# Gates' second half from high and low parts, the ends of two stages reordered, and the first mixture's gathers in another order

## The chip, the cores and the metric

One core of a Trainium2 chip runs the whole program. The metric is the device time of one execution in microseconds (us). TensorE (PE) multiplies, VectorE (DVE), ScalarE (ACT) and GpSimd (POOL) do the rest, SyncE (SP) issues transfers; ScalarE and GpSimd issue some too.

## What is computed

The reference is a chain of six layers on 2048 rows of 256 features, each added to its input: a cross-attention, a delta-rule layer, a mixture of 8 experts, and a second cross-attention, self-attention and mixture. The change touches the second and the third. Cut to what matters:

```python
# L0_attn, the delta-rule layer
q, k, v = (silu(causal_conv(h @ W, conv)) for W, conv in ...)
beta = sigmoid(h @ W_b)
delta_out = delta_rule_chunkwise(q, k, v, beta)      # chunks of 32 rows
fir_s, fir_l = causal_conv(v, short), causal_conv(v, long)
gate_in = concat([h, fir_s, fir_l, delta_out], -1)   # 1024 features
hid = gelu(gate_in @ W_fuse1 + b_fuse1)              # 512 features
logits = (hid @ W_fuse2 + b_fuse2).reshape(b, l, H, 4)
p_raw = sigmoid(logits[..., 3])
floor = 0.01 + 0.09 * (1 - p_raw)
p_val = (1 - floor) * p_raw
others = softmax(logits[..., :3] / exp(others_log_tau))
o = mix of fir_s, fir_l, delta_out, v by others and p_val;  rmsnorm;  @ W_o
# L0_ffn, the first mixture: top 2 of 8 experts, per expert
y = silu(x @ W1[e]) @ W2[e]
```

## The kernel before

Each stage is a block: all engines meet at its end, and within it they run queues written out by hand and held together by semaphores. All sums are kept in f32. PE's matmuls take f32 operands, or, in other stages, a number is split into a high part (rounded to fp32r) and a low part (the rest, in fp32r), and `product3` (L124) makes three fp32r products in place of one f32 product. The copy that rounds is done by ScalarE or GpSimd, the subtraction that leaves the low part mostly by VectorE.

**Work taken ahead.** Layer 4's keys and values for its 64 batches are formed ahead, beside other stages, in parts: three for a batch (`KeysAhead`, from L317; matmuls at L386 and L390, evictions on ScalarE at L410 and L412, then a store, for which the place two batches later waits). `ahead.pe(e, n)` puts n parts into PE's queue, `ahead.act(e, n)` n evictions into ScalarE's. Two banks are used in turn. In the text such a part is a kv part.

**The front of the delta rule** (`delta_attention`, from L992): projections, convolutions, then the norms of q and k in four groups: squares on GpSimd (L1136), sums by PE (`norms`, L1089), a copy by ScalarE (`normed`, L1149), turned by PE (`norms_back`, L1098), taken by VectorE (L1221), square roots on ScalarE (L1199, L1201), reciprocals and two products on VectorE (L1240 to L1248). PE ends with four matmuls without use that keep its clock (L134).

**The solve** (`delta_solve`, from L1256). VectorE solves the triangular systems of 32 rows in two halves, with the taps of the long convolutions (L972) between the steps. SP brings the matrix back turned, in eight loads a half (L1320). PE's queue after the gram matrices is: 14 kv parts, `fuse_most(0)`, 8 kv parts, `half_outputs(0)`, `fuse_rest(0)`, `fuse_most(1)`, `fuse_rest(1)`, 4 kv parts, `fuse_most(2)`, `half_outputs(1)`, `logits(0)`, `fuse_rest(2)`, `fuse_most(3)`, `fuse_rest(3)`, `logits(1)`. `fuse_most(g)` makes, for 512 rows, the first 6 of the 8 chunks of 128 features of gate_in @ W_fuse1, for 4 banks of 128 outputs (L1369, 24 matmuls of 128x512 f32), `fuse_rest(g)` the last 2 (L1375, 8 matmuls), which need the delta rule's output. In the trace each such f32 matmul stands as two records. `half_outputs` multiplies the turned matrix with v (L1350), `hidden(g)` on ScalarE applies gelu (L1438).

**The gates** (`mixture_gates`, from L1524): 16 small steps of VectorE and ScalarE, with 4 kv parts on PE.

**The first mixture** (`experts_0`, from L1740). 23 blocks of rows, in the order narrow (128 rows), wide, wide (256), seven times, and then wide ones. GpSimd gathers for each block 1 MB of W1 (`gather1`, L1849) and 1 MB of W2 (`gather2`, L1855) by the block's expert, and the rows (`gather_rows`, L1868, 128 KB for each half block), all in one queue. For wide blocks GpSimd makes the high part of W1 (`high1`, L1862), VectorE the low one (`low1`, L2077); W2's are made by ScalarE (L2030) and VectorE (`low2`, L2081). There are two slots for the weights and four for the rows. PE turns the rows (L1930) and multiplies with W1 (`hidden`, or `hidden_narrow`, L1942) and W2 (`outputs`). In the text w1(j), w2(j) and rows(j) are the gathers of block j.

## Time and profile before

| | |
|---|---|
| median of 3 runs | 1607.41 us (1605.9 to 1612.63) |
| the profiled execution | 1609.45 us, its span 1607.6 us |
| PE busy | 1484.7 us, 92% of the span |
| VectorE busy | 1097.5 us, 68% |
| ScalarE busy | 813.4 us, 51% |
| GpSimd busy | 586.0 us, 36% |
| mean granted PE clock | 0.986 |
| DMA | 203.99 MB, mean 127 GB/s |

The span runs from the first to the last instruction. Busy time is the time in which at least one instruction of the engine ran. "idle before" names the time that an engine stood before an instruction, and what ended it. A line such as `f_xg<-rows,f_token` gives the output tile and the inputs. The page's clock row, in 40 slices of 40 us, has 9 (nine tenths or more) in all slices but one, which has 8 and begins at 1326 us.

### The profile page before, as it was taken

How to read it: one execution, taken by the hardware profiler on the slowest of the kernel's cores; microseconds unless marked ns; L12 is line 12 of the kernel's file. 1: busy time of each engine (PE TensorE's matmuls, PEld its weight loads, DVE VectorE, ACT ScalarE, POOL GpSimd, SP SyncE). 2: the span in 40 equal slices, each digit the busy share in tenths (PEclk: the TensorE clock that was granted, in tenths of full speed). 3: DMA queues.
4: the chain of work that ended last, by engine and by line, in shares of the span. 5: the costliest groups of instructions: out<-in, count | busy, mean ns of one | idle time of the engine just before them, and what ended most of it. 6: DMA issues, size and time to landing. Idle time of an engine off the chain costs nothing. (4 is left out here: it accounts for less than half of the span.)

```text
span 1607.6 us, 38476 instructions
## 1 busy us (share of the span) xinstructions
PE 1484.7 (92%) x15176; PEld 1139.9 (71%) x15176; DVE 1097.5 (68%) x2412; ACT 813.4 (51%) x1849; POOL 586.0 (36%) x487
## 2 busy tenths in 40 slices
PE   6898989999988889999999889999899788999998
PEld 4454467555456579999998756666688686799997
DVE  4588879973057455566562568888699676767887
ACT  1234742121134336666563548999377322766663
POOL 2440310000011035677654256787388452121210
PEclk9999999999999999999999999999999998999999
DMA  9992059522023367677657417664000000010001
GB/s 321 359 342 74 1 180 215 125 62 46 1 96 122 112 216 253 220 255 253 246 183 189 131 50 245 207 205 135 28 1 1 24 24 15 1 34 21 27 1 53
DMA packets 114075, 203.99 MB, mean 127 GB/s; under 512 B 38074, under 2 KB 74362, under 8 KB 108010
## 3 DMA queue, kind: packets, MB, share of 16 engines
q1 hardware_dynamic: 91481, 107.72, 23.0%
q0 software_dynamic: 10032, 57.55, 10.4%
q10 hardware_dynamic: 12384, 36.27, 6.8%
q8 instruction: 122, 2.00, 0.5%
q14 instruction: 56, 0.45, 0.1%
HBM read 161.67 MB, written 39.83 MB: 125 GB/s over the span
## 5 line engine op out<-in xcount | busy, mean ns | idle before, releaser
L2390 POOL TENSOR_TENSOR a_pr<-a_pr,a_inv 128x1028 f32<-128x1028 f32 x64 | 122.1, 1908 | 58.7 <-DVE a_inv L2523 58.6
L386 PE MATMUL ps<-kv_ctx,kv_w 128*128 128x257 f32 x464 | 120.6, 395 | 9.5 <-PEq L1841 3.1
L2485 ACT ACTIVATE a_pr<-ps,a_neg 128x257 f32<-128x257 f32 x256 | 119.0, 473 | 18.9 <-DVE a_neg L2539 18.8
L390 PE MATMUL ps<-kv_w,kv_ctx 128*128 128x256 f32 x464 | 114.4, 390 | 12.1 <-ACT kv_kv L410 11.5
L1631 POOL TENSOR_TENSOR b0m_pm<-b_dr,b_gates 128x256 f32<-128x256 f32 x16 | 13.2, 831 | 280.5 <-SPq L1595 251.5
L2539 DVE TENSOR_REDUCE a_neg<-ps 128x2 f32<-128x514 f32 x128 | 87.8, 688 | 37.4 <-PE ps L2407 36.4
L390 PEld LDWEIGHTS ps<-kv_w,kv_ctx 128*128 128x128 f32 x464 | 86.7, 193 | 32.3 <-ACT kv_kv L410 20.1
L3401 DVE SCALAR_TENSOR_TENSOR x<-ps,g_gate,x 128x256 f32<-128x256 f32 x256 | 105.1, 475 | 0.0
L386 PEld LDWEIGHTS ps<-kv_ctx,kv_w 128*128 128x128 f32 x464 | 85.5, 195 | 27.5 <-issue 15.0
L972 DVE SCALAR_TENSOR_TENSOR b_F<-b_F,b_fir 128x992 f32<-128x992 f32 (+29 forms) x128 | 96.5, 789 | 0.0
L2418 PE MATMUL ps<-ident,a_pr 128*128 128x128 f32 x512 | 80.4, 279 | 16.0 <-ACT a_prT L2492 10.6
L126 PE MATMUL ps<-gw_w1H,g_hH 128*128 128x256 f32 x320 | 90.6, 283 | 0.8 <-DVE x L3401 0.8
L128 PE MATMUL ps<-gw_w1H,g_hL 128*128 128x256 f32 x320 | 90.5, 283 | 0.0
L127 PE MATMUL ps<-gw_w1L,g_hH 128*128 128x256 f32 x320 | 90.5, 283 | 0.0
L2418 PEld LDWEIGHTS ps<-ident,a_pr 128*128 128x128 f32 x512 | 53.9, 141 | 51.0 <-issue 48.6
L126 PE MATMUL ps<-f_w2H,f0w_hH 128*128 128x256 f32 x312 | 88.6, 284 | 0.2 <-DVE f_w2L L2081 0.2
L128 PE MATMUL ps<-f_w2H,f_hL 128*128 128x256 f32 x312 | 87.9, 282 | 0.0
L127 PE MATMUL ps<-f_w2L,f0w_hH 128*128 128x256 f32 x312 | 87.4, 280 | 0.0
L3371 DVE TENSOR_TENSOR g_hL<-g_hr,g_hH 128x512 fp32r<-128x512 f32 x80 | 57.4, 719 | 39.2 <-ACT g_hH L3339 39.0
L410 ACT ACTIVATE kv_kv<-ps,kv_bk 128x257 f32<-128x257 f32 x92 | 42.5, 471 | 71.6 <-PE ps L386 53.7
L126 PE MATMUL ps<-f_xTH,f0w_w1H 128*128 128x256 f32 x256 | 73.3, 286 | 5.3 <-issue 5.3
L3331 ACT ACTIVATE g_r<-ps 128x512 f32<-128x512 f32 x80 | 47.7, 596 | 53.5 <-PE ps L128 53.5
(448 smaller groups left out, 4431.6 us busy)
## 6 DMA issues: line engine op xcount, KB each, us to landing
late_kv<-kv SPq DMA_DIRECT2D x52, 513.0 KB, 4.1
kv<-kv_kv ACTq DMA_DIRECT2D x46, 513.0 KB
a_ctxT<-in_ctxT SPq DMA_DIRECT2D x32, 514.0 KB, 8.8
a_ctxR<-in_ctx SPq DMA_DIRECT2D x32, 512.0 KB
kv_ctx<-in_ctxT ACTq DMA_DIRECT2D x34, 257.0 KB
kv_ctx<-in_ctxT SPq DMA_DIRECT2D x24, 257.0 KB
outs<-f_yo SPq DMA_DIRECT2D x16, 256.0 KB
a_vB<-vlast SPq DMA_DIRECT2D x32, 128.0 KB
```

What stands on the lines that cost most here:

```text
L126: e.matmul(out, wh, xh, start=start, stop=False)
L127: e.matmul(out, wh, xl, start=False, stop=False)
L128: return e.matmul(out, wl, xh, start=False, stop=stop)
L386: done = e.matmul(out[:, 0:NK], self.w[:, 0, c, cols(part)], ctx[:, c, :], start=(c == 0), stop=(c == DC - 1))
L390: done = e.matmul(out[:, cols(t, D)], ctx[:, c, cols(t)], self.w[:, 1, c, :], start=(c == 0), stop=(c == DC - 1))
L972: return e.scalar_tensor_tensor(acc, x, fir[:, src, at - 1 - sh:at - sh], acc, ALU.mult, ALU.add)
L2390: e.tensor_tensor(pr[:, b % RP, :, :], pr[:, b % RP, :, :], inv[:, b % 2, :].unsqueeze(2).to_broadcast([P, HG, NK]), ALU.mult).then_inc(*p ...
L2418: done = e.transpose(K.ps[:, 6, cols(r)], pr[:, b % RP, r, cols(t)], K.ident[:, :])
L2485: e.activation(pr[:, b % RP, r, :], K.ps[:, bank(b, r), 0:NK], ACT.Exp, bias=neg[:, b % 2, r:r + 1], accum_out=tot[:, b % 2, r:r + 1]).the ...
L2539: e.tensor_reduce(neg[:, b % 2, r:r + 2], K.ps[:, at:at + 2, 0:NK], AX.X, ALU.max, negate=True).then_inc(*v_mx.up())
L3371: e.tensor_tensor(h[1][:, n % HS, :], hr[:, n % 2, :], h[0][:, n % HS, :].bitcast(F32), ALU.subtract).then_inc(*v_l.up())
L3401: done = e.scalar_tensor_tensor(K.x[:, row, :], K.ps[:, 4 + 2 * (m % 2) + half, cols(t, D)], gate[:, row, x - SH:x - SH + 1], K.x[:, row, ...
```

## The change

- The front's end: the sixth kv part comes before `norms(3)` on PE, both last evictions before `normed(3)` on ScalarE, and VectorE's `norms(3)` before the first reciprocal.
- The solve: W_fuse1 is split into `f1H` and `f1L`, and gate_in's chunks for g = 2 and 3 into the two slots of `parts`; for these groups `fuse_parts` makes 3 fp32r matmuls of 128x512 in place of each f32 one, chunk by chunk with the four banks inside (before: bank by bank with the chunks inside). `f1H` takes the place of the keys after the gram matrices, `f1L` that of `f1`, `parts` that of the first two groups of `xnT`. So low parts of the weights can only be made after `fuse_rest(1)`. PE has 12 kv parts before `fuse_most(0)` and 6 after `fuse_rest(1)` (before: 14 and 4).
- Tau's exp and reciprocal move from the gates block to the end of the solve block; the sigmoid becomes exp(-x), + 1, reciprocal.
- The first mixture: GpSimd's queue begins w1(0), w2(0), rows(0), w1(1), rows(1) (before: w1(0), w1(1), w2(0), rows(0), rows(1)).

```diff
@@ delta_attention, tensor
                     norms_back(2)
-                    A.pe(e, 2)
+                    A.pe(e, 3)
                     norms(3)
-                    A.pe(e, 1)
                     norms_back(3)
@@ scalar
-                    A.act(e, 1)
+                    A.act(e, 2)
                     normed(3)
-                    A.act(e, 1)
@@ vector
                     norms(2)
+                    norms(3)
                     e.wait_ge(*a_root.at(1))
                     e.reciprocal(rn[:, 0:12, :], rn[:, 0:12, :]).then_inc(*v_inv.up())
-                    norms(3)
@@ delta_solve, helpers
+        def part(n):
+            return [parts[:, w, cols(n % 2, 512)] for w in range(2)]
+        def low_weights(e, k):
+            if k == 0:
+                e.wait_ge(*a_wh.at(8))
+                e.wait_ge(*t_h.at(8))
+            e.tensor_tensor(f1L[:, k, :], f1[:, k, :], f1H[:, k, :].bitcast(F32), ALU.subtract).then_inc(*v_wl.up())
+        def low_source(e, n):
+            high, low = part(n)
+            e.wait_ge(*a_sh.at(n + 1))
+            e.tensor_tensor(low, source(n % 8, 2 + n // 8), high.bitcast(F32), ALU.subtract).then_inc(*v_sl.up())
@@ tensor
+                def fuse_parts(first, last):
+                    for n in range(first, last):
+                        g, k = 2 + n // 8, n % 8
+                        e.wait_ge(*v_sl.at(n + 1))
+                        if g == 2:
+                            e.wait_ge(*v_wl.at(k + 1))
+                        for m in range(4):
+                            if k == 0:
+                                e.wait_ge(*a_h.at(4 * g + m - 3))
+                            done = product3(e, K.ps[:, m, :], [w[:, k, cols(m)] for w in (f1H, f1L)], part(n), k == 0, k == 7)
+                            if k == 7:
+                                done.then_inc(*t_h.up())
+                        if k < 7:
+                            done.then_inc(*t_k.up())
-                ahead.pe(e, 14)
+                ahead.pe(e, 12)
-                ahead.pe(e, 4)
-                fuse_most(2)
+                ahead.pe(e, 6)
+                fuse_parts(0, 6)
                 ahead.wait_taken(e)
                 half_outputs(1)
                 e.wait_ge(*v_o.at(NT))
                 logits(0)
-                fuse_rest(2)
-                fuse_most(3)
-                fuse_rest(3)
+                fuse_parts(6, 16)
                 logits(1)
@@ scalar
+                def high_source(n):
+                    g, k = 2 + n // 8, n % 8
+                    if n == 0:
+                        e.wait_ge(*t_h.at(8))
+                    if n >= 2:
+                        u = n - 2
+                        if u % 8 == 7:
+                            e.wait_ge(*t_h.at(4 * (2 + u // 8) + 4))
+                        else:
+                            e.wait_ge(*t_k.at(u + 1 - u // 8))
+                    if 2 <= k < 6:
+                        e.wait_ge(*v_fir.at(2 * len(FIR_TAPS)))
+                    if k == 6:
+                        e.wait_ge(*a_oT.at(4 * g + 4))
+                    e.activation(part(n)[0], source(k, g), ACT.Copy).then_inc(*a_sh.up())
-                ahead.act(e, 50)
+                ahead.act(e, 40)
+                e.wait_ge(*ld_f.at(16))
+                e.wait_ge(*t_G.at(NT))
+                for k in range(8):
+                    e.activation(f1H[:, k, :], f1[:, k, :], ACT.Copy).then_inc(*a_wh.up())
+                    ahead.act(e, 1)
...
+                hidden(0)
+                hidden(1)
+                high_source(0)
+                high_source(1)
+                ahead.act(e, 6)
+                for n in range(2, 6):
+                    high_source(n)
+                for t in range(H2, NT):
+                    turned_o(t)
+                for n in range(6, 9):
+                    high_source(n)
+                hidden(2, (0, 1))
+                high_source(9)
+                hidden(2, (2, 3))
+                for n in range(10, 16):
+                    high_source(n)
+                hidden(3)
                 e.wait_ge(*t_lg.at(2))
                 e.activation(lgraw, K.ps[:, 4, :], ACT.Copy).then_inc(*a_raw.up())
+                e.activation(tau[:, :], ltau[:, :], ACT.Exp).then_inc(*a_tau.up())
@@ vector
                 fir_taps(2 * len(FIR_TAPS))
+                for n in range(6):
+                    low_weights(e, n)
+                    low_source(e, n)
+                for k in (6, 7):
+                    low_weights(e, k)
                 for t in range(H2, NT):
                     outputs(t)
+                for n in range(6, 16):
+                    low_source(e, n)
@@ mixture_gates, scalar
-                e.activation(tau[:, :], ltau[:, :], ACT.Exp).then_inc(*a_tau.up())
-                e.activation(raw[:, :, :], lg[:, :, :, 3], ACT.Sigmoid).then_inc(*a_sig.up())
+                e.activation(raw[:, :, :], lg[:, :, :, 3], ACT.Exp, scale=-1.0).then_inc(*a_sig.up())
@@ vector
                 e.wait_ge(*a_sig.at(1))
+                e.tensor_scalar(raw[:, :, :], raw[:, :, :], 1.0, None, ALU.add).then_inc(*v_one.up())
+                e.wait_ge(*v_one.at(1))
+                e.reciprocal(raw[:, :, :], raw[:, :, :]).then_inc(*v_sig.up())
@@ experts_0, gpsimd
                 gather1(0)
-                gather1(1)
+                gather2(0)
                 e.wait_ge(*st_r.at(16 * NT))
-                gather2(0)
                 e.wait_ge(*v_token.at(1))
                 gather_rows(0)
+                gather1(1)
                 gather_rows(1)
                 high1(1)
```

## Rows read from the trace of the kernel before

**Rows 1.** Timeline of TensorE at the front's end: start, duration, what, idle before.

```profile
208.83 1.06 PE L1089 MATMUL ps<-b0a_sq,masks 128*32 128x512 f32 x8 [2.38 <-issue]
...
211.66 0.60 PE L1098 MATMUL ps<-ident,b0a_norm 128*128 128x128 f32 x4
...
216.72 0.26 PE L1334 MATMUL ps<-b_qk 64*32 64x32 f32 x5 [1.02 <-PEq L1033]
```

**Rows 2.** Timeline of TensorE in the solve block.

```profile
292.28 1.99 PE L390 MATMUL ps<-kv_w,kv_ctx 128*128 128x256 f32 x8 [0.54 <-ACT kv_kv L410]
...
330.17 1.93 PE L1350 MATMUL ps<-b_dr,b0s_AS 32*32 32x64 f32 x64 [1.09 <-ACT kv_kv L412]
...
373.72 1.90 PE L386 MATMUL ps<-kv_ctx,kv_w 128*128 128x257 f32 x8
...
378.05 1.88 PE L1369 MATMUL ps<-b_xnT,b0s_f 128*128 128x512 f32 x4
...
398.74 1.10 PE L1350 MATMUL ps<-b_dr,b0s_AS 32*32 32x64 f32 x64
```

**Rows 3.** Timeline of SyncE's queue: the eight loads of the turned matrix, first half.

```profile
317.39 7.22 SPq L1320 DMA_DIRECT2D b0s_AS<-turned  x8
```

**Rows 4.** View of line L1320: time from issue to landing, 16 loads.

```profile
DMA to landing us min/median/max: 2.2/3.6/4.3
```

**Rows 5.** Timeline of TensorE in the last mixture, three fp32r matmuls of 128x512 apart.

```profile
1402.06 0.40 PE L126 MATMUL ps<-g_xnH,gw_w1H 128*128 128x512 f32 x1
...
1402.75 0.28 PE L126 MATMUL ps<-gw_w1H,g_hH 128*128 128x256 f32 x1
```

**Rows 6.** Groups by line and shape: count | busy us, mean ns | idle before.

```profile
L3371 DVE TENSOR_TENSOR g_hL<-g_hr,g_hH 128x512 fp32r<-128x512 f32 x80 | 57.4, 719 | 39.2 <-ACT g_hH L3339 39.0
...
L3339 ACT ACTIVATE g_hH<-g_hr 128x512 fp32r<-128x512 f32 x80 | 50.6, 633 | 2.6
```

**Rows 7.** Timeline of ScalarE and TensorE in the gates block.

```profile
450.91 1.28 ACT L1543 ACT_TABLE_LOAD   x1 [1.52 <-PEq L1301]
...
456.22 3.24 PE L386 MATMUL ps<-kv_ctx,kv_w 128*128 128x257 f32 x8 [2.44 <-ACT kv_kv L410]
...
460.28 0.84 PE L1603 MATMUL ps<-ident,b_F 128*128 128x128 f32 x6 [0.82 <-PEq L1536]
```

**Rows 8.** Timeline of GpSimd in the first mixture.

```profile
593.93 1.89 POOL L1862 CAST f0w_w1H<-f_raw 128x2048 fp32r<-128x2048 f32 x1 [1.70 <-DMA f_raw<-in_L_ffn_W1T,f_wrow]
595.98 3.08 POOL L1868 DMA_INDIRECT f_xg<-rows,f_token  x1 [0.16 <-issue]
...
606.35 0.94 POOL L1849 DMA_INDIRECT f_raw<-in_L_ffn_W1T,f_wrow  x1 [4.80 <-PE ps L1942]
...
612.69 1.90 POOL L1862 CAST f0w_w1H<-f_raw 128x2048 fp32r<-128x2048 f32 x1 [4.14 <-DMA f_raw<-in_L_ffn_W1T,f_wrow]
...
638.49 1.01 POOL L1849 DMA_INDIRECT f_raw<-in_L_ffn_W1T,f_wrow  x1 [0.30 <-issue]
...
646.38 1.89 POOL L1862 CAST f0w_w1H<-f_raw 128x2048 fp32r<-128x2048 f32 x1 [3.94 <-DMA f_raw<-in_L_ffn_W1T,f_wrow]
...
678.08 1.91 POOL L1862 CAST f0w_w1H<-f_raw 128x2048 fp32r<-128x2048 f32 x1 [4.99 <-DMA f_raw<-in_L_ffn_W1T,f_wrow]
```

**Rows 9.** Timeline of TensorE in the first mixture.

```profile
599.04 0.69 PE L1930 MATMUL ps<-ident,f_xg 128*128 128x128 f32 x2 [7.23 <-DMA f_xg<-rows,f_token]
...
632.72 3.74 PE L1942 MATMUL ps<-f_xN,f_raw 128*128 128x128 f32 x32
...
663.00 3.74 PE L1942 MATMUL ps<-f_xN,f_raw 128*128 128x128 f32 x32
...
714.33 0.36 PE L126 MATMUL ps<-f_xTH,f0w_w1H 128*128 128x256 f32 x1 [1.42 <-issue]
```

**Rows 10.** Timeline of VectorE beside the second row of rows 8.

```profile
595.92 2.29 DVE L2077 TENSOR_TENSOR f0w_w1L<-f_raw,f0w_w1H 128x2048 fp32r<-128x2048 f32 x1 [6.38 <-POOL f0w_w1H L1862]
```

**Rows 11.** Busy time by stretch: PE, PEld, DVE, ACT, POOL, granted clock, DMA.

```profile
327.00:329.00 2.00, 2.00 (x6) 1.11 (x4) 0.00 (x0) 0.00 (x0) 0.00 (x0) 0.52 0.47 127
```

More of the change, by code:

```diff
@@ L996, in delta_attention @@
         sb = Y.sb
-        xnT = sb("xnT", [P, DC, ROWS])
+        with Room(Y, "b0x") as Z:
+            xnT = Z.sb("xnT", [P, DC, ROWS])
+        parts = sb("parts", [P, DC, ROWS], F32R)
+        with Room(Y, "b0k") as Z:
+            kk = Z.sb("kk", [P, 2, ROWS])
+        f1H = sb("f1H", [P, 8, 512], F32R)
         wo = sb("wo", [P, DC, D])
@@ L1250, in delta_attention, with delta_solve @@
         K.front.Y.close()
-        delta_solve(K, A, a_first, xnT, qk, F, fir, dr, rn, cb, ab, f2, bf1, bf2, lg, ld_2)
-        mixture_gates(K, A, lg, gates, ltau)
+        tau = sb("tau", [P, H0])
+        delta_solve(K, A, a_first, tau, ltau, xnT, parts, qq, kk, f1H, F, fir, dr, rn, cb, ab, f2, bf1, bf2, lg, ld_2)
+        mixture_gates(K, A, lg, gates, tau)
         delta_mix(K, A, F, dr, gates, wo, nw)
-def delta_solve(K, ahead, a_first, xnT, qk, F, fir, dr, rn, cb, ab, f2, bf1, bf2, lg, ld_2):
+def delta_solve(K, ahead, a_first, tau, ltau, xnT, parts, qq, kk, f1H, F, fir, dr, rn, cb, ab, f2, bf1, bf2, lg, ld_2):
     H2 = NT // 2
@@ L1266, in delta_solve @@
         step = sb("step", [P, L * L // 4])
-        f1 = sb("f1", [P, 8, 512])
+        with Room(Y, "b0f") as Z:
+            f1 = Z.sb("f1", [P, 8, 512])
+        f1L = sb("f1L", [P, 8, 512], F32R)
         ld_f, d_AS, d_Mt = Y.sigs_of("dma", "f1 AS Mt")
+        a_wh, a_sh = Y.sigs_of("act", "fhigh shigh")
+        v_wl, v_sl, t_k = Y.sig("dve", "flow"), Y.sig("dve", "slow"), Y.sig("pe", "chunk")
         ld_A, d_M = ([Y.sig("dma", f"{n}{h}") for h in range(2)] for n in "AM")
@@ L1333, in grams @@
                             out, col = K.ps[L * b:L * b + L, 2 * s + h % 2, :], L * (h // 2)
[L1334 removed]
+                            e.matmul(out[:, col:col + L], kk[rows, h // 2, at], kk[rows, h // 2, at],
                                      start=True, stop=True)
[L1336 removed]
+                            e.matmul(out[:, P + col:P + col + L], kk[rows, h // 2, at], qq[rows, h // 2, at],
                                      start=True, stop=True)
@@ L1427, in _, with hidden @@
             def _(e):
+                def high_source(n):
[13 more added lines that the diff above has]
+                    e.activation(part(n)[0], source(k, g), ACT.Copy).then_inc(*a_sh.up())
                 def turned_o(t):
                     e.wait_ge(*t_oT.at(t + 1))
-                    e.activation(qk[:, 0:2, cols(t)], K.ps[:, 6 + t % 2, 0:D].rearrange(
+                    e.activation(qq[:, 0:2, cols(t)], K.ps[:, 6 + t % 2, 0:D].rearrange(
                         "p (c n) -> p c n", c=DC), ACT.Copy).then_inc(*a_oT.up())
-                def hidden(g):
-                    for m in range(4):
+                def hidden(g, ms=range(4)):
+                    for m in ms:
                         e.wait_ge(*t_h.at(4 * g + m + 1))
@@ L1446, in _ @@
                     turned_o(t)
-                for g in range(NG):
-                    if g == 2:
-                        ahead.act(e, 4)
-                        for t in range(H2, NT):
-                            turned_o(t)
-                    hidden(g)
+                hidden(0)
[15 more added lines that the diff above has]
+                hidden(3)
                 e.wait_ge(*t_lg.at(2))
                 e.activation(lgraw, K.ps[:, 4, :], ACT.Copy).then_inc(*a_raw.up())
+                e.activation(tau[:, :], ltau[:, :], ACT.Exp).then_inc(*a_tau.up())
             @block.vector
@@ L1517, in _, with mixture_gates @@
                 fir_taps(2 * len(FIR_TAPS))
+                for n in range(6):
[3 more added lines that the diff above has]
+                    low_weights(e, k)
                 for t in range(H2, NT):
                     outputs(t)
+                for n in range(6, 16):
+                    low_source(e, n)
                 e.wait_ge(*ld_2.at(96))
                 logits()
-def mixture_gates(K, ahead, lg, gates, ltau):
+                e.wait_ge(*a_tau.at(1))
+                e.reciprocal(tau[:, :], tau[:, :])
+def mixture_gates(K, ahead, lg, gates, tau):
     with Layer(K, "b0g") as Y:
         raw, fl, mx, tot = (Y.sb(n, [P, NT, H0]) for n in ("raw", "fl", "mx", "tot"))
-        tau = Y.sb("tau", [P, H0])
         oth = Y.sb("oth", [P, NT, H0, 3])
-        a_sig, a_tau, a_exp = Y.sigs_of("act", "sig tau exp")
-        v_itau, v_scl, v_max, v_sub, v_sum, v_inv, v_floor, v_pval, v_rest, v_scale = Y.sigs_of(
-            "dve", "itau scl max sub sum inv floor pval rest scale")
+        a_sig, a_exp = Y.sigs_of("act", "sig exp")
+        v_one, v_sig, v_scl, v_max, v_sub, v_sum, v_inv, v_floor, v_pval, v_rest, v_scale = Y.sigs_of(
+            "dve", "one sig scl max sub sum inv floor pval rest scale")
         def over(t):
@@ L1550, in _ @@
             def _(e):
-                e.wait_ge(*a_tau.at(1))
-                e.reciprocal(tau[:, :], tau[:, :]).then_inc(*v_itau.up())
-                e.wait_ge(*v_itau.at(1))
                 e.tensor_tensor(oth[:, :, :, :], lg[:, :, :, 0:3],
```

13 lines of the change are left out of this document (6 added, 7 removed).

## The prediction

> **What bounds the kernel now.** I read the busy shares first: TensorE (PE) is busy for 92% of the span and holds its full clock in nearly every slice, so only what shortens PE's own queue, or a wait in it, can pay. Then I read the timelines of the three stretches that the change touches, to see who sets each of them. At the end of the delta rule's front (to 216.7 us) the next block starts when VectorE and ScalarE have finished a chain that hangs on PE's last norm step; PE stands for 2.38 us before it [rows 1]. In the solve block (216.7 to 450.9) PE runs without a gap through the gates' hidden layer, 24 matmuls for each run from 378.05 to 398.74 [rows 2]. The gates block (450.9 to 460.3) is led by ScalarE's table loads [rows 7]. In the first mixture (from 599.04) PE looks full, but its gather queue on GpSimd (POOL) repeats at 31.7 us per three blocks (646.38 to 678.08, both the same step of the loop) [rows 8], while PE needs 30.3 us for three blocks (632.72 to 663.00); at 714.33 PE waits 1.42 us for a weight half that has just been finished [rows 9]. So there the loader is the bound from the fifth block on, and PE only the follower.
>
> **The end of the front.** The sixth kv part moves ahead of norms(3) and norms_back(3). It takes PE 1.8 us and fits the 2.38 us that PE idles before norms(3) [rows 1], which waits for POOL's squares and so doesn't move. norms_back(3), at 211.66, can then follow ScalarE's copy directly, at about 210.6. Behind it, PE still has four clock-keeping matmuls (3.6 us), which end at 214.8 instead of 215.7. VectorE's chain, which ended last at 216.4, gets its norms(3) before the first reciprocal and ends by 214. The next block starts about 0.3 us after the last engine: 215.1 instead of 216.72 [rows 1]. **Gain 1.6 us**, bounds 0 and 2.
>
> **The solve block.** (a) Two kv parts leave the place before fuse_most(0). Four of them take 4.3 us from 373.72 to 378.05, so two cost 2.2, and the wait of 0.54 before 292.28 goes with them: 2.7 us [rows 2]. But half_outputs(0), at 330.17, needs the turned M as well. SP issues those eight loads in 7.22 us from 317.39, and each lands 2.2 to 4.3 us after its issue [rows 3, 4], so the last is there at about 328. VectorE's solve, which sets that time, isn't touched by this edit. The eight f1H copies that ScalarE puts between kv evictions (0.63 us each, the row of the like copy [rows 6]) stay under the same cover. I take 2.1 of the 2.7; bounds 0 and 2.7. (b) The same two parts come back after fuse_rest(1), where 4 parts take 373.72 to 378.05 [rows 2]: with 6 parts, and half a microsecond for ScalarE, which first does hidden(1)'s last part and two copies, this is 7.3 us, a cost of 3.0. That is also the cover under which VectorE makes its first low halves. (c) The matmuls. A 128x512 f32 matmul costs (398.74 - 378.05) / 24 = 0.86 us [rows 2]. Three fp32r matmuls of the same size start 0.69 us apart (1402.06 to 1402.75) [rows 5]. For g = 2 and 3 there are 2 x 4 x 8 = 64 of them: 64 x (0.86 - 0.69) = 10.9 us gained, if PE never waits for parts. The parts cost 24 ScalarE copies of 0.63 and 24 VectorE subtractions of 0.72 [rows 6]; both engines are nearly idle in 378 to 398 and in 411 to 445. With two slots, the turn is: PE ends a chunk, copy 0.63, subtraction 0.72, and 0.3 for the hand-offs, 1.65 us, against the 2.8 us of the other chunk (12 matmuls). So 1.1 us of slack per chunk. At the change from g = 2 to g = 3, high_source(9) stands between the halves of hidden(2), and PE's third and fourth bank of chunk 8 wait for those: 0.2 us. Before half_outputs(1), VectorE also has low_weights 6 and 7 (1.4 us), done while PE works on chunk 5. logits(0), 3.6 us of PE, hides high_source(6) and low_source(6). (d) ScalarE's Exp of tau, with its table load of 1.28 (the row of its present place [rows 7]), now ends the block: it runs beside the last transposes and VectorE's logits, and comes out 0.5 us behind them. Sum of the block: -2.1 + 3.0 - 10.9 + 0.2 + 0.5 = **-9.3 us**. Bounds -12 and -4; the far one has PE waiting 0.3 us in each chunk.
>
> **The gates block.** Before: three table loads in a row (one row stands for those at 450.91, 452.43 and 454.06), then the kv evictions, so PE's third and fourth part start at 456.22 after 2.44 us of wait and take 3.24 at the reduced clock; the next block starts at 460.28 [rows 7]. After: only Exp is used and its table is already there. The two added VectorE steps (+1 and a reciprocal, 0.2 and 0.55) lie beside the kv parts. PE needs about 4.6 us for four parts at full clock, and the last eviction, hand-off and block change take 1.2 more: 5.9 us instead of 9.4, **gain 3.4**. Bounds 1.5 and 4.
> The Trainium skill (ScalarE activation tables, Table sets in the compiler and the runtime) says that loads are placed per block, which speaks against this edit: Exp at the head of a new block would be loaded again. No row here has the same table on both sides of a block change. By that rule and the load's 1.28 in the trace, this block gives 0.7 less, and the forecast would be 1596.3.
>
> **The gathers.** Now the queue is w1(0), w1(1), w2(0), rows(0), rows(1); it becomes w1(0), w2(0), rows(0), w1(1), rows(1). PE's first transpose, at 599.04 after 7.23 us of wait [rows 9], comes behind 2 MB of weights instead of 3. The second MB had landed at 593.93 [rows 8], so PE starts near 594.5: **4.5 us earlier for PE**. But high1(1), on POOL, waits for w1(1), which is now the third MB: it starts at about 599.3 instead of 593.93. Queued behind it on POOL are both halves of rows(2), w2(1) and w1(2). The first takes 3.08 us instead of 0.95, since VectorE's low1(1) runs beside it (595.98 against 595.92 [rows 8, 10]), and will again. So w2(1) is issued at 606.0, 5.4 later, and w1(2) right behind it at 607.3, where it now stands alone, at 606.35, gated by PE [rows 8]. Two weights one behind the other: from 638.49, the issue of the second, with the first 3.3 before it, to 646.38 is 7.9 us [rows 8]. That puts w1(2) at 615.4 instead of 612.69: 2.7 us late. hidden(2) can still start a microsecond early, but the loader's next rounds hang on this landing: w1(3), w2(2) and w1(4) follow in the same queue, then high1(4), w1(5), high1(5). hidden(5) has only 0.5 us of slack today, and hidden(8) and hidden(11) none. So PE's early start ends in waits at blocks 2, 5 and 8, and the mixture ends as late as its loader: **+2.5 us**. Bounds: -4.5 (PE's start, if the loader catches up) and +4.4 (if w1(3)'s issue is stretched by low1(2) as well).
> The Trainium skill (SBUF — State Buffer, Who interferes with whom) infers that a tensor_tensor of VectorE leaves the descriptor writing of GpSimd's DMAs alone. The trace disagrees: 3.08 us beside one [rows 8, 10] and 0.94 at 606.35 without [rows 8]. By the rule w1(2) would be 2 us sooner, and the forecast 1593.6.
>
> **The sum.** -1.6 - 9.3 - 3.4 + 2.5 = -11.8 us. The profiled execution has a span of 1607.6 us and took 1609.45; the runs' median is 1607.41. The differences are taken from rows of that execution and put on the median: **1595.6 us**.
>
> **Rivals.**
> 1. *The loader catches up.* PE's 4.5 us hold: 1607.4 - 14.3 - 4.5 = 1589. For it: the loader has waits of 3 to 5 us for landings in each round, which shorter queues might use, and w1(2) is no longer gated by PE. Against: the 31.7 us against 30.3.
> 2. *The parts come too slowly.* The turn of 1.65 us is over 2.8 only if neighbours in the queues intrude (low_weights on VectorE, hidden on ScalarE). At half a microsecond of wait in 14 chunks, 7 us are lost: 1603. Against: the slack of 1.1.
> 3. *The other side: the clock falls in the product loop.* After waits of PE of 2 to 3 us the granted clock was 0.52 of full, its lower level of 1.2 GHz (327 to 329 [rows 11]). A chunk's twelve matmuls would take 5.2 us instead of 2.8. All 16 chunks at it cost 38 us: 1634. It decides from 5 chunks on (11.8 / 2.4), and from 9 on the kernel is slower by over 0.5%. Against: before those chunks PE has 7 us of kv parts without a wait, and the page's clock row shows no fall in today's long runs of matmuls.
> 4. *A saving isn't there*: the tables are loaded again and the turned M lands no sooner (2.8 less), within the range.
>
> **How the numbers follow.** Forecast (loader sets the mixture, product loop without waits) 0.54, with 1592 to 1601 as its own range; rival 1 0.27; rival 2 0.14; rival 3 0.05. Range 1587 to 1602: rival 1 less 2, to the forecast with the bound +4.4 and a microsecond; rival 3 and the slow part of rival 2 are left out. A measurement of this kernel tells 0.5%, 8 us, from no change; faster means under 1599.4. From the cases: faster 0.50 + 0.27 + 0.02 = 0.79; same 0.04 + 0.12 + 0.01 = 0.17; slower 0.04.
>
> **What would show it.** Right: the block after the front starts near 215; 64 groups of three matmuls 0.7 apart with no wait for low_source; two table loads fewer in all, and the gates block under 6.5 us; PE's first transpose of the mixture 4 to 5 us after the token is there, with new waits of PE at blocks 2 and 5, and a mixture that is 1 to 4 us longer from token to end. Wrong: waits of PE on VectorE in the product loop (rival 2), a clock under 1.00 there (rival 3), or a mixture shorter by 4 us (rival 1).

## The result and the profile after

The changed kernel took **1602.38 us** (median of 20 runs, 1590.27 to 1610.65), the kernel before 1610.94 us (20 runs, 1603.01 to 1623.69). The ratio is **0.9948** (95% interval 0.9927 to 0.9969): 8.4 us less, between 5.0 and 11.8. Predicted were 1595.6 us and 11.8 us less. Two later comparisons gave 0.991 (0.9876 to 0.9944) and 0.995 (0.993 to 0.9969), see e1 and e13. Executions over 1.5% above the fastest of their kernel are left out of the ratios and of the spans below; the profiled executions of e3 and e7 are such ones. The profiled execution took 1599.07 us, its span is 1597.3 us, 10.3 less than before's.

The busy shares hardly differ: TensorE (PE) is at 92% again.

```profile
PE 1474.0 (92%) x15240; PEld 1151.7 (72%) x15240; DVE 1115.1 (70%) x2438; ACT 824.4 (52%) x1871; POOL 582.5 (36%) x487
```

**The front's end and the solve block.** Timeline of PE after the change: start, duration, what, idle before. The last row is the first of `logits(1)`.

```profile
209.05 1.06 PE L1094 MATMUL ps<-b0a_sq,masks 128*32 128x512 f32 x8 [0.65 <-issue]
210.88 0.66 PE L1103 MATMUL ps<-ident,b0a_norm 128*128 128x128 f32 x4 [0.77 <-ACT b0a_norm L1153]
...
215.27 0.26 PE L1357 MATMUL ps<-b0k_kk 64*32 64x32 f32 x5 [0.30 <-PEq L1038]
...
318.99 1.03 PE L386 MATMUL ps<-kv_ctx,kv_w 128*128 128x257 f32 x4
326.88 1.93 PE L1373 MATMUL ps<-b_dr,b0s_AS 32*32 32x64 f32 x64 [6.86 <-issue]
...
370.69 1.03 PE L386 MATMUL ps<-kv_ctx,kv_w 128*128 128x257 f32 x4
...
377.58 0.58 PE L126 MATMUL ps<-b_parts,b_f1H 128*128 128x512 f32 x1
...
394.51 1.10 PE L1373 MATMUL ps<-b_dr,b0s_AS 32*32 32x64 f32 x64
...
405.93 0.50 PE L126 MATMUL ps<-b_parts,b_f1H 128*128 128x512 f32 x1
...
434.05 0.62 PE L1421 MATMUL ps<-b0s_A,b_f 128*32 128x512 f32 x1
```

The wait of 2.38 us before the norms is 0.65, and the next block starts at 215.27 instead of 216.72 [rows 1]. half_outputs(0) starts at 326.88 instead of 330.17 [rows 2], but now after 6.86 us of waiting: PE is done with its kv parts at 320, and the loads of the turned M are issued late on SyncE's queue, 5.35 us behind the store instead of the 2.62 before (start, duration, what):

```profile
311.82 0.33 SPq L1340 DMA_DIRECT2D turned<-b0s_M  x1
317.17 5.14 SPq L1343 DMA_DIRECT2D b0s_AS<-turned  x8
```

The first half of the new products takes 16.93 us (377.58 to 394.51) where 24 f32 matmuls took 20.69 [rows 2], with no wait in it. The groups of that stretch (count | busy us, mean ns | idle before) show 24 products of three matmuls and no idle time:

```profile
L128 PE MATMUL ps<-b_parts,b0s_f1L 128*128 128x512 f32 x24 | 9.5, 398 | 0.0
L126 PE MATMUL ps<-b_parts,b_f1H 128*128 128x512 f32 x24 | 9.5, 397 | 0.0
L127 PE MATMUL ps<-b_parts,b_f1H 128*128 128x512 f32 x24 | 9.4, 392 | 0.0
```

**The gates block.** Timeline of ScalarE: one table load is left, ahead of the block, and the Exp at its head (L1620) has none, against the load at 450.91 and two more behind it [rows 7].

```profile
438.34 1.28 ACT L1523 ACT_TABLE_LOAD   x1
439.63 0.21 ACT L1523 ACTIVATE b_tau<-b_ltau 128x4 f32<-128x4 f32 x1
440.33 0.32 ACT L1620 ACTIVATE b0g_raw<-b_lg 128x64 f32<-128x64 f32 x1 [0.49 <-PEq L1324]
441.52 0.36 ACT L1622 ACTIVATE b0g_oth<-b0g_oth 128x192 f32<-128x192 f32 x1 [0.88 <-DVE b0g_oth L1632]
```

**The first mixture.** Timeline of GpSimd (POOL), then of PE. The first rows' gather is issued at 578.25; in the trace of before it was at 588.77.

```profile
578.25 0.94 POOL L1945 DMA_INDIRECT f_xg<-rows,f_token  x1 [7.43 <-DVE f_token L2278]
579.50 0.94 POOL L1926 DMA_INDIRECT f_raw<-in_L_ffn_W1T,f_wrow  x1 [0.30 <-issue]
580.74 0.95 POOL L1945 DMA_INDIRECT f_xg<-rows,f_token  x1 [0.30 <-issue]
582.00 0.95 POOL L1945 DMA_INDIRECT f_xg<-rows,f_token  x1 [0.30 <-issue]
586.88 1.89 POOL L1939 CAST f0w_w1H<-f_raw 128x2048 fp32r<-128x2048 f32 x1 [3.94 <-DMA f_raw<-in_L_ffn_W1T,f_wrow]
588.93 3.08 POOL L1945 DMA_INDIRECT f_xg<-rows,f_token  x1 [0.16 <-issue]
...
594.88 0.94 POOL L1926 DMA_INDIRECT f_raw<-in_L_ffn_W1T,f_wrow  x1 [0.30 <-issue]
...
607.17 1.89 POOL L1939 CAST f0w_w1H<-f_raw 128x2048 fp32r<-128x2048 f32 x1 [10.09 <-DMA f_raw<-in_L_ffn_W1T,f_wrow]
```

```profile
584.32 0.44 PE L2007 MATMUL ps<-ident,f_xg 128*128 128x128 f32 x2 [1.88 <-DMA f_xg<-rows,f_token]
...
589.98 0.66 PE L2007 MATMUL ps<-ident,f_xg 128*128 128x128 f32 x4 [0.78 <-DMA f_xg<-rows,f_token]
...
599.40 0.66 PE L2007 MATMUL ps<-ident,f_xg 128*128 128x128 f32 x4 [3.42 <-DMA f_xg<-rows,f_token]
...
611.49 0.55 PE L126 MATMUL ps<-f_xTH,f0w_w1H 128*128 128x256 f32 x1 [2.68 <-issue]
```

PE's first transpose comes 6.07 us after that issue instead of 10.27 [rows 9]. But three waits follow that were not there: for the rows of block 1 (at 589.98, 0.78), for those of block 2 (at 599.40, 3.42) and for block 2's weights (at 611.49, 2.68).

### The profile page after: what moved, and what is told of

The parts are those of the page before. It is cut to its first block and busy times, and to the rows that moved or that the text cites. A ratio compares the mean times of both kernels' runs of the same rounds, so it can differ in the third digit from the quotient of the medians.

```text
span 1597.3 us, 38672 instructions
## 1 busy us (share of the span) xinstructions
PE 1474.0 (92%) x15240; PEld 1151.7 (72%) x15240; DVE 1115.1 (70%) x2438; ACT 824.4 (52%) x1871; POOL 582.5 (36%) x487
## 5 line engine op out<-in xcount | busy, mean ns | idle before, releaser
L2495 PE MATMUL ps<-ident,a_pr 128*128 128x128 f32 x512 | 81.1, 281 | 15.8 <-ACT a_prT L2569 10.6
L2154 DVE TENSOR_TENSOR f0w_w1L<-f_raw,f0w_w1H 128x2048 fp32r<-128x2048 f32 x16 | 36.7, 2292 | 62.7 <-POOL f0w_w1H L1939 62.7
```

What stands on the lines that cost most here:

```text
L2495: done = e.transpose(K.ps[:, 6, cols(r)], pr[:, b % RP, r, cols(t)], K.ident[:, :])
```

## The experiments

Each kernel was timed with the kernel before beside it on the same chip. Two measures are used. One is the length of a stage, read from the starts on PE and POOL in each timeline; it is not brought to an equal clock unless that is said. The other is the mean span at an equal granted clock: over 211 executions a span was 1.26 us shorter for each 0.001 that its mean granted clock was higher (slope within kernels), and spans were brought to 0.980 with it; what is left is 1.0 to 1.5 us of uncertainty (one standard error) for each kernel. All uncertainties in us below are of this kind. A stage length comes from one execution of each kernel.

| kernel | ratio (95%) | against before, equal clock |
|---|---|---|
| e1, the changed kernel again | 0.991 (0.9876 to 0.9944) | -11.3 |
| e2, old gathers | 0.9899 (0.9857 to 0.994) | -15.5 |
| e3, f32 products | 1.0026 (0.9992 to 1.0059) | +5.1 |
| e4, old gates block | 0.9978 (0.995 to 1.0006) | -8.2 |
| e5, before with new gathers | 1.0048 (0.9998 to 1.0099) | +8.4 |
| e6, w2(1) and w1(2) early | 0.995 (0.9912 to 0.9987) | -10.7 |
| e7, two kv parts earlier | 0.9923 (0.9883 to 0.9963) | -10.6 |
| e8, tau early | 0.9938 (0.99 to 0.9976) | -11.1 |
| e9, rows first | 0.9902 (0.9866 to 0.9939) | -14.4 |
| e10, rows first, tau early | 0.9912 (0.9878 to 0.9947) | -13.3 |
| e11, old gathers, clock kept | 0.9874 (0.9838 to 0.9911) | -17.5 |
| e12, e11 and tau early | 0.9885 (0.9857 to 0.9913) | -15.3 |
| e13, the changed kernel again | 0.995 (0.993 to 0.9969) | -8.4 |
| e14, old gathers | 0.9943 (0.9928 to 0.9957) | -10.8 |

e1 to e4 ran on one chip, e5 to e8 together, e9 to e11 together, e12 to e14 together.

### e1 and e13: the changed kernel

> The changed kernel once more, so that the runs beside it have their own measure on the same chip. From the two traces the change takes 13.0 us off up to the block behind the gates, 1.7 us of it go again to a lower clock ahead of the router, and the first mixture takes as long as before: 10 us in all, a ratio of 0.994. If the profiled execution was a lucky one, the ratio is nearer to 0.996 (6 us).

> The changed kernel beside the next run and the one before it. From the first rows' gather to the last output weights 260 to 267 us as in the seven profiles of the new order so far, PE waits of 1 us or more for rows(1) and rows(2), and 0.2 to 3.5 us for w1(2) at block 2.

At equal clock the changed kernel is 11.3 and 8.4 us faster than the kernel before; each difference has some 1.5 us of uncertainty, so the two agree. The mean granted clock of the kernel before was 0.9795 over 24 runs and 0.9796 over 15, that of the changed kernel 0.9812 and 0.9787: the change neither costs nor gives clock as a whole. In e13 PE waited 4.09 us for the rows of block 2 and 0.95 for its weights, but not for the rows of block 1, which the expectation had.

### e2 and e14: the old order of the gathers

```diff
-                gather2(0)
+                gather1(1)
                 e.wait_ge(*st_r.at(16 * NT))
+                gather2(0)
                 e.wait_ge(*v_token.at(1))
                 gather_rows(0)
-                gather1(1)
```

> The changed kernel with the old order of the gathers (w1(0), w1(1), w2(0), then the rows). By the prediction the new order costs 2.5 us, so this kernel would be 2.5 us faster than the changed one. By rival 1 (the loader catches up and PE's early start holds) it would be 4.5 us slower. From the trace after, the theory is now that neither holds: the start is 4.2 us earlier, the wait at block 2 takes 2.7 of it, the third and later rounds of the loader take the rest, and both orders end the mixture within 1 us of each other. Then this kernel is within 1 us of the changed one; its first transpose of the mixture comes 10.3 us after the issue of the first rows' gather instead of 6.1, PE has no wait at block 2, and waits of 0.8 to 2 us at blocks 8, 11, 14 and 17.

> The changed kernel with the old order of the gathers alone. If the new order costs 2.5 us (the prediction) to 4.8 us (the means of the profiles so far, three against seven), this kernel is faster than the changed one beside it by that, and its stretch from the first rows' gather to the last output weights takes 254 to 261 us. If the means of the profiles came from their spread, the two kernels' times and stretches overlap.

Against the changed kernel beside them they are 4.2 us and 2.4 us faster at equal clock (each about 1.9 uncertain). The stage from the first rows' gather to the last output weights took 261.1, 259.8, 254.1, 255.6 and 260.0 us in the five profiles of the old order (before, e2, e11, e12, e14; mean 258.1) and 260.3, 265.3, 263.8, 266.8, 260.7 and 263.3 in six of the new one (after, e1, e4, e5, e8, e13; mean 263.4). Of the old ones, e11 and e12 have other edits too; without them the mean is 260.3 and the difference 3.1. So the new order costs 3 to 5 us by the stages and 2 to 4 by these times, and my theory from the first pair of traces, that it costs nothing, falls: that pair was the new order's shortest against the old one's longest. Most of it is lost early. The hidden layer of block 4 starts 53.6, 53.8 and 54.1 us after the first rows' gather in before, e2 and e14, and 56.1, 54.8, 55.8, 56.0, 57.8 and 57.0 us after it in the six of the new order: 2.4 us later in the mean, although PE's first transpose comes 3 to 6 us sooner.

Timeline of PE in e2, old order: the start is late, and PE has no wait from there to block 8, where it waits 1.03 us for weights (block 1's hidden layer starts at 597.36).

```profile
584.55 0.69 PE L2007 MATMUL ps<-ident,f_xg 128*128 128x128 f32 x2 [7.68 <-DMA f_xg<-rows,f_token]
...
591.23 0.60 PE L2007 MATMUL ps<-ident,f_xg 128*128 128x128 f32 x4
...
597.01 0.60 PE L2007 MATMUL ps<-ident,f_xg 128*128 128x128 f32 x4
```

### e5: the new order alone, on the kernel before

The diff of e2 backwards, in the kernel before.

> The kernel before with the new order of the gathers alone. In the profiles so far the stretch from the first rows' gather to the last block's output weights took 260.3, 265.3, 262.1 and 263.8 us with the new order and 261.1 and 259.8 with the old one, so the prediction's +2.5 us is still in play. If it holds, this stretch takes 262 to 265 us here, PE waits 2 to 4 us for the weights of block 2, and the kernel is 2.5 us slower than the kernel before (ratio 1.0015). If the new order costs nothing, the stretch takes 259 to 261 us. If PE's early start holds (rival 1), it is 4.5 us shorter, under 257 us.

It is the slowest of all: +8.4 us at equal clock, and its stage took 266.8 us. PE waited 5.54 us for the rows of block 2, then 1.10, 0.64, 2.09, 1.60 and 1.72 us for weights at blocks 5, 8, 11, 17 and 20. With e2 and e14, the order of the gathers costs between 2 and 8 us; the direction is the same in all three comparisons, though only e5 is far outside its uncertainty (1.4 us; e2 and e14 have 1.9).

### e3: f32 products

```diff
-                fuse_parts(0, 6)
+                fuse_most(2)
...
-                fuse_parts(6, 16)
+                fuse_rest(2)
+                fuse_most(3)
+                fuse_rest(3)
```

The copies high_source and the subtractions low_source and low_weights are left out with it; the eight copies to f1H stay.

> The changed kernel with the second half of the gates' hidden layer in plain f32 again (no parts made on ScalarE and VectorE), everything else as changed. Theory (the prediction's term): 64 places of 0.86 us instead of 0.69, 10.2 to 10.9 us slower than the changed kernel, ratio to the kernel before 1.000 to 1.001; the stretches are 20.7 us and 34.5 us long instead of 16.9 and 28.1. Rival: the engines that make the parts cost something elsewhere (clock or shared memory), then the loss is under 8 us.

The two stages took 20.69 and 34.53 us, against 16.92 and 28.12 in e1 beside it: 10.2 us, as the theory has it. By the spans it is 16.4 us (1.7 uncertain) slower than e1 and 15 slower than the mean of e1 and e13. The rival (a loss under 8) is out. Why the spans show some 5 us more than the two stages stays open.

### e4: the old gates block

```diff
-                e.activation(tau[:, :], ltau[:, :], ACT.Exp).then_inc(*a_tau.up())
...
-                e.activation(raw[:, :, :], lg[:, :, :, 3], ACT.Exp, scale=-1.0).then_inc(*a_sig.up())
+                e.activation(tau[:, :], ltau[:, :], ACT.Exp).then_inc(*a_tau.up())
+                e.activation(raw[:, :, :], lg[:, :, :, 3], ACT.Sigmoid).then_inc(*a_sig.up())
```

> The changed kernel with the old gates block: Exp of tau, Sigmoid and Exp with their three table loads at its head, no Exp of tau in the solve block. By the prediction the edit gave 3.4 - 0.5 = 2.9 us, so this kernel is 2.9 us slower. From the traces it gave 1.7 us, since PE's clock was at its lower level for the first parts (441 to 443 us). If that low clock comes with the longer stop of PE ahead of the block (1.32 us instead of 0.85), it is full here at the block's head and the kernel 1.7 us slower; if the low clock comes whatever the stop, it is low here too and the kernel is 2.9 us slower.

3.1 us slower than e1 at equal clock (1.6 uncertain). Busy time and granted clock (after the five engines' busy times) of the gates block in before, after, e1 and e4:

```profile
450.95:460.28 9.33, 6.07 (x21) 4.32 (x21) 3.45 (x12) 6.50 (x10) 0.02 (x1) 0.82 0.25 85
```
```profile
440.35:447.51 7.16, 6.34 (x20) 4.80 (x21) 3.84 (x13) 2.68 (x6) 0.01 (x1) 0.76 0.20 59
```
```profile
444.27:449.75 5.48, 4.66 (x21) 3.64 (x21) 3.85 (x13) 2.57 (x6) 0.02 (x1) 1.00 0.28 80
```
```profile
441.56:449.63 8.07, 4.81 (x21) 3.63 (x21) 3.46 (x12) 6.49 (x10) 0.02 (x1) 1.00 0.28 98
```

The same code takes 7.16 us with a granted clock of 0.76 and 5.48 at 1.00, the old one 9.33 and 8.07. At equal clock the edit gives 2.6 us in the block, and less the 0.47 of the tau step, 2.1 in all. The longer stop of PE ahead of the block does not alone bring the low clock: that stop is the same in after and e1. Of the sixteen profiles the block has the low clock in five of the ten with the stop of 1.32 us (after, e3, e9, e13, e14) and in one of the six with a shorter one (before). That is too few to say whether the stop makes it likelier; which executions are hit is open.

### e6: w2(1) and w1(2) issued early

```diff
                 gather_rows(1)
+                gather2(1)
                 high1(1)
+                gather1(2)
...
```

The loop behind it leaves these two out.

> The changed kernel with two of POOL's gathers moved up: w2(1) is issued ahead of high1(1), and w1(2) right behind high1(1) and ahead of rows(2). If the wait at block 2 comes from the late issue of w2(1) and w1(2) (the prediction's step), w1(2) is issued some 5 us sooner, is there by about 20 us after the first rows' gather (29 in the changed kernel), the wait of 2.7 us at block 2 goes, and the stretch from the first rows' gather to the last block's output weights is 2.5 to 4 us shorter than in the changed kernel. If the later rounds of the loader are the bound whatever its start, PE waits more at blocks 8 and 11 and the stretch stays at 260 to 262 us.

The wait at block 2 is gone and the stage took 259.3 us, 4 less than the mean of the new order. PE still waited 2.12 and 3.62 us for the rows of blocks 1 and 2; those of block 1 are behind w1(1) and those of block 2 behind high1(1) as in the changed kernel. The two kinds of wait are separate. The spans (-10.7 against -11.3 of e1) don't show the gain.

### e9 and e10: rows first

```diff
                 gather1(0)
-                gather2(0)
+                gather1(1)
                 e.wait_ge(*st_r.at(16 * NT))
                 e.wait_ge(*v_token.at(1))
-                gather_rows(0)
-                gather1(1)
-                gather_rows(1)
+                for j in range(3):
+                    gather_rows(j)
+                gather2(0)
+                gather2(1)
                 high1(1)
+                gather1(2)
...
```

The loop behind it leaves these out. e10 has the edit of e8 besides.

> The changed kernel with a third order of the gathers: w1(0) and w1(1) ahead of the token as in the kernel before, then the rows of blocks 0, 1 and 2, then w2(0) and w2(1), then high1(1) and w1(2). Theory: the first transpose needs only 2 MB of weights ahead of its rows (this gave 4.2 us), and the waits that took this gain in the changed kernel (3 to 5 us for rows(2), queued on POOL behind the wait for w1(1), and 0.2 to 3.5 us at block 2 for w1(2)) go, as nothing now waits behind w1(1). From the first rows' gather to the last output weights: 254 to 257 us, against 263 (mean of seven profiles) with the new order and 260.4 (mean of two) with the old one. Rival: the loader's rounds of 30.9 to 32 us against PE's 30.3 are the bound, and the early start is given back at blocks 5 to 17; then 258 to 261 us.

> The same with the Exp of tau ahead of the copy of the logits (0.4 us in the profile of that edit alone). As a whole it should be 7 to 9 us faster than the changed kernel if the theory of the gathers holds, a ratio to the kernel before of 0.988 to 0.990; if the loader is the bound, 2 to 4 us faster, 0.991 to 0.993.

The stage took 257.3 and 257.7 us. The early start holds (6.8 and 5.2 us from the first rows' gather) and no wait for rows is left but one of 0.49 in e10, so the queue behind w1(1) and high1(1) was their cause. PE's first transpose in e9 (timeline):

```profile
580.78 0.44 PE L2009 MATMUL ps<-ident,f_xg 128*128 128x128 f32 x2 [4.22 <-DMA f_xg<-rows,f_token]
```

Later it waits for weights instead: 0.27, 1.40, 0.51, 0.69, 0.53, 1.42 and 0.29 us at blocks 2, 5, 8, 11, 14, 17 and 20, and in e10 3.02 us at block 2. The stage is between theory (254 to 257) and rival (258 to 261): 6 us less than the new order, but not the sum of both gains; the loader takes a part. The spans are 14.4 and 13.3 us below the kernel before, so 2 to 6 us better than the changed kernel and not the 7 to 9 of the theory, and no better than the old order (15.5 and 10.8 us in e2 and e14). In e9, w1(2) is issued when low1(1) is over, and its gather took 0.95 us on POOL; in e10 it ran beside low1(1) and took 3.05 us, as the rows' gather did in the changed kernel (3.08).

### e7: two kv parts earlier

```diff
-                ahead.pe(e, 8)
+                ahead.pe(e, 10)
...
-                ahead.pe(e, 6)
+                ahead.pe(e, 4)
...
```

ScalarE's evictions move with them.

> The changed kernel with two kv parts moved from behind fuse_rest(1) to behind fuse_most(0), where PE stood for 6.9 us in the first trace after. If the turned M is what half_outputs(0) waits for, the parts fit into this wait and the block is 2.5 us shorter (4.3 us instead of 6.9 behind fuse_rest(1)), and the first low halves are still ready. If the evictions on ScalarE and their stores set it, as in the four profiles of the runs before (wait for the last eviction 1.2 to 1.9 us), half_outputs(0) comes 2 to 4 us later and the block is as long as now or 1 us longer.

Behind fuse_rest(1) the parts took 4.86 us instead of 6.89, but half_outputs(0) came 20.35 us after the end of fuse_most(0) instead of 18.47 in after, and the spans show no gain (-10.6 against -11.3 in e1). PE still waited 4.3 us there for the turned M, whose loads in SyncE's queue (timeline) began 5.7 us after its store, late as in after (311.82 to 317.17). Up to fuse_rest(0) the block took 124.8 us, against 122.9 in the mean of the five other profiles of the new block with late loads (see the solve term in the next section): the 2.0 us gained behind fuse_rest(1) went again here.

```profile
315.44 0.33 SPq L1340 DMA_DIRECT2D turned<-b0s_M  x1
321.17 5.87 SPq L1343 DMA_DIRECT2D b0s_AS<-turned  x8
```

### e8: tau early

```diff
                 hidden(3)
+                e.activation(tau[:, :], ltau[:, :], ACT.Exp).then_inc(*a_tau.up())
                 e.wait_ge(*t_lg.at(2))
                 e.activation(lgraw, K.ps[:, 4, :], ACT.Copy).then_inc(*a_raw.up())
-                e.activation(tau[:, :], ltau[:, :], ACT.Exp).then_inc(*a_tau.up())
```

> The changed kernel with ScalarE's Exp of tau issued ahead of the copy of the gates' logits instead of behind it. By the prediction's step (d) this Exp with its table load ends the block 0.5 us late; here it runs while PE multiplies the logits, and from the first logits(1) matmul to the gates block it takes 5.8 us again instead of 6.3. The copy of the logits is not delayed, and no further table load comes with it. Nothing else moves: 0.5 us, which the times can't tell from the changed kernel.

From logits(1) to the gates block: 5.90 us, against 6.30. No further table load came with it.

### e11 and e12: the clock kept ahead of half_outputs(0)

e11 is e2 with one line more, e12 is e11 with the edit of e8.

```diff
                 ahead.wait_taken(e)
+                keep_clock(K, e, 6, 4)
                 half_outputs(0)
```

> The changed kernel with the old order of the gathers, and four products without use (128x512 f32, 0.86 us each) on PE between the last eviction of kv and half_outputs(0), where PE stood for 4 to 7 us in three of the profiles with the clock at its lower level behind it. Theory: where the turned M is late, the products cost nothing, and half_outputs(0) takes 7.8 us at the full clock instead of 9.3 to 9.8. Where the last eviction is late, they delay half_outputs(0) by up to 3.5 us. The mixture's stretch from the first rows' gather to the last output weights is 259 to 262 us, as with the old order so far; with the new one it was 260.3 to 266.8.

> The changed kernel with what gained in the runs before: the old order of the gathers, the four products without use ahead of half_outputs(0), and the Exp of tau ahead of the copy of the logits. Expected 3 to 6 us faster than the changed kernel beside it (2.5 to 5 from the gathers, 0.4 from tau, up to 1.7 from the clock where the turned M is late), a ratio to the kernel before of 0.987 to 0.990. If the gathers' order makes no difference, 1 to 2 us faster.

Timeline of PE in e11:

```profile
328.86 3.70 PE L134 MATMUL ps<-masks,ident 128*128 128x512 f32 x8 [1.27 <-ACT kv_kv L410]
333.83 1.10 PE L1373 MATMUL ps<-b_dr,b0s_AS 32*32 32x64 f32 x64 [1.27 <-DMA b0s_AS<-turned]
```

The first 64 products of half_outputs(0) take 1.10 us instead of the 1.93 of after, the whole 7.77 instead of 9.47, and the turned M is still late, so the four products cost nothing here. In e12 the loads came 2.62 us behind the store, and the products cost:

```profile
328.83 3.70 PE L134 MATMUL ps<-masks,ident 128*128 128x512 f32 x8 [1.48 <-ACT kv_kv L410]
```

half_outputs(0) follows them at 332.46 without a wait, and up to fuse_rest(0) the block took 122.0 us, against 119.1 in the mean of the six profiles of the new block without the products in which the loads came as soon.

e11 and e12 are the fastest kernels: 0.9874 and 0.9885. e12 is 6.9 us faster than e13 beside it at equal clock, and its interval (0.9857 to 0.9913) lies below that of the changed kernel (0.993 to 0.9969). That is more than the 0.4 of tau and the 2.4 of e14's gathers, and the products cannot be its cause in this profile. Its mixture took 255.6 us with no wait of PE from block 1 on. Whether an edit in the solve block can help the mixture, or its loader was lucky in e11 and e12, is not settled.

## Why the prediction was right or wrong

Four of its seven terms were right, three mis-sized. The time (1602.38) lies 0.4 us outside the range of 1587 to 1602. The forecast difference (11.8 us) lies at the edge of the measured 5.0 to 11.8. The time missed by 6.8 us: 3.5 are the base, the rest are terms that were too favourable, above all the gathers. There a wait had been left out: PE stops for rows that are queued behind high1(1), 3.4 to 5.5 us in six profiles.

- **Front's end, -1.6.** Right: 42.05 us from the first norms to the next block before, 40.38 after, 1.67 less. All executions that had the full clock there repeat it to 0.02.
- **Solve (a), -2.1, bounds 0 and 2.7.** From the grams to fuse_rest(0) it is 122.7 and 121.1 us in the two kernels with the old block (before, e5) and 117.7 to 124.6 in ten with the new one, mean 121.0: about -0.9. The first pair of traces alone has 1.6. What failed is the landing of the turned M "at about 328" as one fixed time. In after the store came 1.5 us sooner than the front's end explains, and the loads 2.7 us later behind it (5.35 us instead of 2.62). The profiles fall into two groups. Where the loads come 2.6 to 2.9 us behind the store, the new block takes 119.1 us (six profiles: e1, e2, e3, e4, e6, e9), which is 2.8 less than the old one, or 2.3 if half_outputs(0) is put at its 7.77 us at the full clock in before and e4 (9.21 and 9.04 there): the term and its far bound have it so. Where they come 4.7 to 5.7 us behind it, it takes 122.9 (after, e8, e10, e13, e14). Both profiles of the old block are of the first group; two are too few to say whether the change makes the second likelier.
- **(b) +3.0.** Right in kind: 6.89 us instead of 4.33, +2.56.
- **(c) -10.9 +0.2.** Right: 3.76 and 6.41, 10.2 us; the products start 0.69 apart, and neither slots nor low halves made PE wait. The rest to 10.9 lies in 0.4 us at the change from kv parts to products and in a few tenths inside the second stretch. Rivals 2 and 3 are out: no waits, and a granted clock of 1.00 in both stages.
- **(d) +0.5.** Right: +0.47, and e8 takes 0.4 back.
- **Gates block, -3.4.** Mis-sized: 2.6 at equal clock. The step that failed set 9.4 us "at the reduced clock" against 5.9 at the full one. The clock of that execution isn't the edit's gain; e4 shows 8.07 for the old block without it.
- **The tables.** The Trainium skill (ScalarE activation tables: per-element evaluation and per-set limits, Table sets in the compiler and the runtime) has loads placed per block. By that rule the gates block would have been 0.7 us longer than forecast. The trace has no load at the head of the gates block, after Exp was loaded at the end of the block before, so the trace disagrees.
- **Gathers, +2.5, bounds -4.5 and +4.4.** The sign was right, the size too small: 3 to 5 us by the stages, 2.4 to 8.4 by the spans. PE's start came 4.2 us earlier (4.5 predicted). The step that failed is "hidden(2) can still start a microsecond early": on PE's queue turn(2) stands ahead of hidden(1), so rows(2), queued on POOL behind high1(1), stop block 1 and not block 2. PE waited 3.4 to 5.5 us there in after, e1, e3, e4, e5 and e13; in e7 and e8 rows(2) were in time (a wait of 0.4 and none), and it waited 3.3 and 3.0 us for rows(3), which stand ahead of hidden(2) in the same way. These waits are in no step. Moving the rows ahead of high1(1) (e9, e10) took them away.
- **Gathers, what else was off.** A second step was mis-sized: w1(2) was issued 16.6 us after the first rows' gather (18.5 predicted) but cast at 28.9 (26.6), so it took 12.3 us from its issue and not 8.1; why is open. The forecast waits at block 5 came in e1, e4, e5 and e13 (0.7 to 1.7 us), not in after and e8, and in no profile of the old order, so the late loader takes a part as well. Two smaller terms were left out. The first rows' gather comes 0.76 us after the last write of the token instead of 0.27, in all eleven profiles in which the waits for the store and for the token stand one behind the other, against the five in which w2(0) is between them. And behind the new waits the granted clock fell to its lower level: in after it was 0.53 from 611.0 to 614.6, and the first products of block 2 start 0.64 us apart instead of 0.36, some 1.4 us in all.
- **The descriptors.** The Trainium skill (SBUF — State Buffer, Who interferes with whom) infers that a tensor_tensor leaves the descriptor writing alone; the trace disagrees again, 3.08 us beside one (588.93) and 0.95 in e9, where it was over.
- **Rival 1, the loader catches up.** Not as written: the start was lost. But the loader's round isn't the fixed 31.7 us of one pair of rows: in after the same step came at 638.25, 670.38, 701.54, 732.32 and 762.68, so 32.1, 31.2, 30.8 and 30.4 us.
- **The base.** The differences were put on 1607.41, a median of three runs; 20 runs give 1610.94. The profiled execution of before had a mean granted clock of 0.986 where 24 others had 0.9795, and this clock alone is worth 8 us at 1.26 us for each 0.001. On 1610.94 the same sum gives 1599.1. With the terms as the stages measured them (-1.7, -0.9, +2.6, -10.2, +0.5, -2.6 and +3.1 to +5) it is 7.3 to 9.2 us less than the kernel before, 1601.7 to 1603.6; measured were 8.4 and 1602.38.

## What to carry to other kernels

When a transfer is moved ahead in a queue, walk the queues of its consumers too: the wait that matters is the first one in program order that needs anything behind the moved transfer, not the one of the block that it feeds. Compare stages only at the same granted clock, and take a stage's length and the base time from several executions before a term of 1 to 3 us is trusted. Products without use ahead of a late input keep the clock (1.7 us in e11), but where the input is in time they only delay (some 3 us in e12): count first how often it is late, here in seven of sixteen profiles.

## What was new about the hardware

- Three fp32r matmuls of 128x512 take 0.69 us also where their parts are made just ahead: ScalarE's copies (626 to 630 ns) and VectorE's subtractions (688 to 693 ns) ran beside them without a wait of PE.
- The same gates block ran with a granted clock of 0.76 and of 1.00 in executions with the same instructions and the same waits ahead; the span follows the mean granted clock by 1.26 us for each 0.001, which accounts for about half of the variance between the executions of a kernel.
- The table of Exp that ScalarE loaded in one block (438.34) was still there in the next: no load ahead of the Exp at 440.33.
- The store of the turned M and the first of its loads were 2.6 to 2.9 us apart on SyncE's queue in nine profiles and 4.7 to 5.7 us in seven (after, e7, e8, e10, e11, e13, e14), and the same kernel had both (after 5.4, e1 2.6, e13 5.1). What delays the store's landing is open.
- An indirect gather of 128 rows took 0.95 us on POOL, and 3.05 or 3.08 us when it was issued just behind the start of VectorE's 2.29 us subtraction (e10 at 594.56, after at 588.93).
